# Perceiver block on one core: row loads issued ahead of the given chunks, statistics two tiles later, a third bank for the turned keys

## Time and profile before

| | us |
|---|---|
| median of 3 runs (lowest, highest) | 682.21 (680.39, 685.39) |
| the profiled execution | 680.11 |
| its span, first to last instruction | 678.4 |
| PE busy | 590.3 |
| DVE busy | 416.3 |
| ACT busy | 218.7 |
| POOL busy | 194.1 |
| granted TensorE clock, mean | 0.945 |

### The profile page before, as it was taken

The page is one execution under the profiler, slowest core; times in us unless marked ns, Lnnn a source line. Parts: engine busy times, 40 slices in busy tenths (PEclk is TensorE's granted clock), DMA queues, the critical chain, the costliest instruction groups (busy, mean ns, idle before and its releaser), DMA issues.

```text
span 678.4 us, 13117 instructions
## 1 busy us (share of the span) xinstructions
PE 590.3 (87%) x5217; PEld 365.4 (54%) x5217; DVE 416.3 (61%) x1026; ACT 218.7 (32%) x515; POOL 194.1 (29%) x259
## 2 busy tenths in 40 slices
PE   6999978979797978899687889999999999998778
PEld 5654444434343433444375576674958567584645
DVE  3967577867777685873658564563828264473732
ACT  0321231616252532233121243251516234151412
POOL 0423386775867576550000000101000010101010
PEclk9999969979897989799897799999999999999989
DMA  8960789593979776659606301203030301203000
GB/s 305 374 213 0 272 349 349 188 359 125 394 254 369 256 287 236 238 190 370 236 30 188 93 2 63 49 1 111 1 95 16 94 18 61 50 2 99 13 16 15
DMA packets 58972, 108.24 MB, mean 160 GB/s; under 512 B 19984, under 2 KB 22560, under 8 KB 56864
## 3 DMA queue, kind: packets, MB, share of 16 engines
q1 hardware_dynamic: 58912, 107.41, 45.4%
HBM read 96.91 MB, written 10.49 MB: 158 GB/s over the span
## 4 chain that ended last, share of the span: by engine, by line
PE 42%; issue 33%; DMA 8%; DVE 8%; POOL 3%; ACT 3%; SPq 1%; DVEq 0%; ACTq 0%; POOLq 0%
PE u_ps L878 8%; PE s_ps L852 7%; DMA area<-in_ctx_dram 7%; PE bank L943 3%; PE bank L817 3%; PE s_ps L725 2%; PE bank L1023 2%; PE max_ps L867 2%; PE s_ps L758 2%; DVE area L1396 1%; POOL area L491 1%; DMA area<-in_L_xattn_ln_b_dram 1%; DVE area L1117 1%; PE bank L1053 1%; PE max_ps L1023 1%
## 5 line engine op out<-in xcount | busy, mean ns | idle before, releaser
L1117 DVE BATCH_NORM_STATS2 area<-area 128x6 f32<-128x384 f32 (+1 forms) x208 | 104.2, 542 | 25.4 <-DMA area<-in_ctx_dram 25.4
L491 POOL TENSOR_SCALAR area<-area 128x384 f32<-128x384 f32 (+1 forms) x160 | 105.9, 673 | 10.3 <-POOL area L484 10.3
L878 PE MATMUL u_ps<-area,yT_all 128*64 128x384 f32 (+1 forms) x416 | 85.1, 539 | 0.7 <-ACT yT_all L609 0.7
L484 POOL TENSOR_TENSOR area<-area,minus_half 128x4 f32<-128x4 f32 (+1 forms) x56 | 56.2, 1003 | 99.9 <-DVE area L1126 99.9
L527 POOL TENSOR_TENSOR area<-area,minus_half 128x1 f32<-128x1 f32 x8 | 4.3, 539 | 240.0 <-DVE area L1390 240.0
L852 PE MATMUL s_ps<-area 128*64 128x512 f32 x288 | 69.9, 622 | 0.0
L999 PE MATMUL u_ps<-area 128*128 128x512 f16 x256 | 60.5, 386 | 0.0
L583 ACT COPY area<-bank 128x384 f32<-128x384 f32 (+1 forms) x80 | 32.1, 455 | 60.0 <-PE bank L817 60.0
L1412 DVE COPY area<-s_ps 128x512 f32<-128x512 f32 x8 | 5.5, 691 | 69.3 <-PE s_ps L1011 69.3
L878 PEld LDWEIGHTS u_ps<-area,yT_all 128*64 128x64 f32 (+1 forms) x416 | 27.5, 145 | 32.1 <-issue 30.4
L852 PEld LDWEIGHTS s_ps<-area 128*64 128x64 f32 x288 | 22.0, 148 | 41.5 <-issue 40.7
(11 more groups left out here) (181 smaller groups left out, 1021.2 us busy)
## 6 DMA issues: line engine op xcount, KB each, us to landing
area<-in_ctx_dram SPq DMA_DIRECT2D x96, 384.0 KB, 7.3
area<-in_ctx_turned_dram SPq DMA_DIRECT2D x32, 768.0 KB, 7.0
area<-in_L_ffn_W_turned_dram SPq DMA_DIRECT2D x16, 1024.0 KB, 8.7
skew<-area SPq DMA_DIRECT2D x8, 1024.0 KB, 4.3
area<-skew SPq DMA_DIRECT2D x16, 256.0 KB, 4.7
x_sb<-in_x_dram SPq DMA_DIRECT2D x8, 256.0 KB, 8.4
out_dram<-area SPq DMA_DIRECT2D x8, 256.0 KB, 2.0
area<-in_ctx_dram SPq DMA_DIRECT2D x16, 97.5 KB
```

The lines of the kernel that those rows point to most:

```text
L484: pool.tensor_tensor(rs[b][:, sl], ve[b][:, sl], minus_half[:, 0:n], ALU.pow).then_inc(s["rstd_ready"], 1)
L491: pool.tensor_scalar(raw[b][0:m, u, j, :], raw[b][0:m, u, j, :], negmu[b][0:m, i:i + 1], rs[b][0:m, i:i + 1], ALU.add, ALU.mult).then_inc( ...
L878: ins = pe.matmul(u_ps[u * L:(u + 1) * L, 0:DC], pT[0:m, j % NSLOT, u * L:(u + 1) * L], raw[b][0:m, u, j, :], start=(j == 0), stop=(j == N ...
L1117: dve.bn_stats(st[b][0:m, stat_at(u, j), :], raw[b][0:m, u, j, :]).then_inc(s["key_stats_done"], 1)
```

## The change

- SP issues the given chunk 2 of pair p - 1 not ahead of k = 0 of pair p, but behind its k = 1; the given chunk 1 of p goes behind k = 4 instead of k = 2. Of the last pair, chunk 2 is issued behind the loop.
- LEAD becomes 4 and STATS_AT [2, 2, 2, 2, 1, 2, 2]: step 0 does tiles 4 and 5, steps 1 to 3 the same tiles as before, step 4 tile 12 alone, step 5 tiles 0 and 1 of the next pair, step 6 tiles 2 and 3.
- The turned tiles rotate through three banks; the third is the bank of the factors. A turn waits for the copy three before it. A turn into the third bank also waits until the factors of the earlier pair (for tile 12: of this pair) are copied out, and the spreading of factors waits until the eight turns of chunk 0 are copied out.

```diff
-    LEAD = 6
+    LEAD = 4
-    STATS_AT = [0, 2, 2, 2, 2, 2, 3]
+    STATS_AT = [2, 2, 2, 2, 1, 2, 2]
...
-        tbank = [bank[0], bank[1]]
+        tbank = [bank[0], bank[1], s_ps[:, 1536:2048]]
...
-            load_given(1, 2)
             for p in range(2, NP):
                 for k in range(NL):
                     load_next(p, k)
-                    if k == 2:
+                    if k == 1:
+                        load_given(p - 1, 2)
+                    if k == 4:
                         load_given(p, 1)
                     if p in (4, 5) and k in (2, 5):
                         load_for_sum(2 * p - 4 + (k - 2) // 3)
-                load_given(p, 2)
+            load_given(NP - 1, 2)
...
-                             tbank[i % 2][:, 0:KC * P]...
+                             tbank[i % 3][:, 0:KC * P]...
...
-                    at_least(pe, s["turned_copied"], i - 1)
+                    at_least(pe, s["turned_copied"], i - 2)
+                    if i % 3 == 2:
+                        if p == 0:
+                            pe.wait_ge(s["cq_sums"], NT)
+                        at_least(pe, s["factors_copied"], len(GIVEN) * (p + (j == FT)))
...
                 pe.wait_ge(s["rstd_ready"], NB * p + 2 * ch + 2)
+                pe.wait_ge(s["turned_copied"], 2 * (len(TURNED) * p + len(TURNED) - 1))
                 at_least(pe, s["factors_copied"], i)
```

More of the change, by code:

```diff
@@ L583, in evacuate @@
                     act.copy(slot(j // CH)[:, u, :, (j % CH) * P:(j % CH) * P + m],
-                             tbank[i % 2][:, 0:KC * P].rearrange("p (c k) -> p c k", c=KC)[:, :, 0:m]).then_inc(s["turned_copied"], 1)
+                             tbank[i % 3][:, 0:KC * P].rearrange("p (c k) -> p c k", c=KC)[:, :, 0:m]).then_inc(s["turned_copied"], 1)
             def factors_out(p, ch):
@@ L814, in turn @@
                         pe.wait_ge(s["key_normed"], POOL_NORMS * p + 3 * g + 2 * (j % 2) + u + 1)
-                    at_least(pe, s["turned_copied"], i - 1)
+                    at_least(pe, s["turned_copied"], i - 2)
[3 more added lines that the diff above has]
+                        at_least(pe, s["factors_copied"], len(GIVEN) * (p + (j == FT)))
                     for c in range(KC):
-                        ins = pe.transpose(tbank[i % 2][:, c * P:c * P + m], raw[b][0:m, u, j, c * P:(c + 1) * P], ident_f[0:m, 0:m])
+                        ins = pe.transpose(tbank[i % 3][:, c * P:c * P + m], raw[b][0:m, u, j, c * P:(c + 1) * P], ident_f[0:m, 0:m])
                     ins.then_inc(s["key_turned"], 1)
```

## The result

| | before | after |
|---|---|---|
| median of the runs, us | 681.74 (680.39 to 685.39, 4 runs) | 652.62 (650.78 to 654.40, 4 runs) |
| profiled execution, us | 680.11 | 650.78 |
| its span, us | 678.4 | 649.1 |
| granted TensorE clock, mean | 0.945 | 0.966 |

The ratio of the times, after to before, is 0.9565, with a 95% interval of 0.9515 to 0.9615. A second timing of the same kernel gave 650.60 us and 0.9534 (0.9491 to 0.9577). The forecast was 650 and faster.

The account below looks back on a forecast made before the run. PE was taken as nearly the bound, with 6.4 us per pair lost preparing the next pair. Savings of 32.8 and 2.5 us less 4.2 gave 31.1, so 680.1 became 649.0 profiled, stated as 650 median; forecast 643 to 656, range 641 to 666.

Parts of the forecast that it names:

- What bounds the kernel: Pairs' loop: PE nearly the bound; preparing the next pair adds about 6.4 us per pair in waits and slow clock.
- The stall of 3.2 us: PE at L867: starts 3.2 us late because statistics waiting for rows precede chunk 1's maximum; moving them later removes it.
- DVE's step 0, no cost: DVE's step 0: an added 2.6 us statistics group costs nothing; context copy done at T + 7.5 instead of T + 7.2.
- The third bank, 0.3 us: PE's turned tiles: a third bank removes two 0.39 us waits per pair, counted as 0.3 us; bounds 0 to 0.8.
- The given chunk, 0.7 us in each of six stretches: PE before scoring chunk 2, stretches 1 to 6: new 0.7 us wait each, 4.2 in all; bounds 0 to 1.5.
- The sum: Whole run: 32.8 us from pairs 2 to 7, 2.5 from pair 1, less 4.2 for chunk waits: 31.1 us saved.
- The other signs: Trace after: L867 wait under 1 us, DVE's row wait below 8, stretches about 27.5, clock above 0.97, chunk wait near 4.
- (a): Rival, chance 0.16: DVE becomes the bound, its own norms held by POOL, 2.2 us per pair lost: 663 us.
- (b): Rival, chance 0.11: rows still late, k = 3 and given chunk slip 2 to 3 us per pair: 665 us.
- (c): Rival, chance 0.05: given chunk 2 lands so late that its wait exceeds the gain, slower: 689 us.
- (d): Rival, chance 0.05: nothing moves, chunk 1's maximum waits for the factors' copy instead: 678 us.
- (e): Rival, chance 0.05: better, no wait for the given chunk and pair 1 fully regained: 641.5 us.

Follow-up runs that it names:

- experiment 10: Changed kernel with STATS_AT = [2, 1, 3, 2, 1, 2, 2] and given chunk 2 issued behind k = 0: 644.51 us; the same with two banks: 647.69 us.
- the two experiments with one edit each: Kernel before with only the new LEAD and STATS_AT: 659.57 us; kernel before with only the new order of loads: 658.80 us.
- experiment 5: Changed kernel with the loads in their old order, keeping the later statistics and third bank: 669.02 us, ratio 0.9853.
- Experiment 7: Changed kernel with STATS_AT = [2, 1, 3, 2, 1, 2, 2], one tile instead of two ahead of step 1's context copy: 647.36 us, ratio 0.9523.
- experiment 8: Changed kernel with the given chunk 2 issued behind k = 0 instead of k = 1: 647.95 us, ratio 0.9535.
- experiment 6: Changed kernel with two banks for the turned keys instead of three: 652.44 us, ratio 0.9570.
- experiments 3: Kernel before with the third bank alone, and the waits that belong to it: 675.48 us, ratio 0.9920.
- experiment 9: Changed kernel with the given chunk 2 issued behind k = 2 instead of k = 1: 676.84 us, ratio 0.9911.

## Why the prediction was right

*What bounds the kernel.* Right. The time of a stretch without a next pair was the measure of what the others could reach, and experiment 10 reaches it within 0.3 us.

*The stall of 3.2 us.* Right, and the two experiments with one edit each show that either removes it. The prediction put it down to the statistics' place and counted nothing for the loads but their price. That was half of it: in experiment 5, with the old order, DVE waits 1.0 to 3.3 us for k = 3 in four of the stretches. The prediction had no term for this; of chunk 1's new place it said only "lands 10 us early".

*DVE's step 0, no cost.* The moment was right, the price wasn't, and this is where one of the prediction's own signs of being wrong came: DVE's context copy stands among what PE waits for, 8.6 us in seven. PE in stretches 3 and 4 of the kernel after:

```profile
149.12 0.80 PE L906 MATMUL max_ps<-ident_f,area 128*128 128x128 f32 x3 [1.17 <-DVE area L1258]
...
178.58 0.52 PE L906 MATMUL max_ps<-ident_f,area 128*128 128x128 f32 x3 [1.76 <-DVE area L1258]
```

Stretch 3 starts at 141.63, so the context is turned at T + 7.49, where T + 7.5 was forecast, and so it is in five of the stretches 2 to 7; stretch 4 starts at 170.55 and is late, at T + 8.03. Of that 0.5 us, 0.3 is a short DVE instruction (L1132) that takes 0.48 us instead of 0.17, until POOL's norms end. But a longer wait there isn't only its own time. After stretch 3's the clock is down, at 1.2 GHz:

```profile
150.00:151.00 1.00, 1.00 (x4) 0.39 (x6) 1.00 (x5) 1.00 (x2) 0.93 (x2) 0.50 0.25 55
```

That happened in stretches 3 and 5 (28.9 and 28.4 us, clock 0.94) and not in the others; in the second timing's profile it was stretches 3 and 4. The sum took the clock as 1.00 from stretch 2 on; this is the term that was too good, by about 3.2 us (PE busy 27.2 and 27.1 us in these two, 25.5 at the full clock). Experiment 7 takes 0.5 us off each of these waits, and the clock stays up in stretches 2 to 7, as it does in both kernels of experiment 10; in experiment 8, where the waits are as long as here, it falls in stretches 2 and 5. That supports the link. But experiment 8 and the three-bank kernel of experiment 10 have the clock at 0.88 in stretch 1, where no context is turned, so this wait is not all that a fall can come behind; and why waits of 1.2 us are followed by a fall in two stretches of six and not in the rest is not explained.

*The third bank, 0.3 us.* Right in stretch 7 (26.9 us without it in experiment 6, 26.6 with it), for the reason given: DVE's context copy caps it. The whole time can't show so small a term. Without the cap it is 0.7 (stretch 7 of experiments 3 and 10). "The new waits cost nothing" was wrong for pair 0, whose tile 12 comes right behind the spreading of chunk 2's factors, with no probabilities to turn and no tiles to weight in between:

```profile
84.36 0.37 PE L822 MATMUL s_ps<-ident_f,area 65*128 65x65 f32 x3 [0.78 <-ACT area L592]
```

*The given chunk, 0.7 us in each of six stretches.* Right in kind, 2.9 us instead of 4.2: three waits, of 0.62, 0.44 and 1.81 us, the last in stretch 4 with its weight pieces. The chain of waits shows that one: SP needs 0.8 us for k = 1, from 186.06, and 1.9 us (of which 1.37 for its first DMA) for the chunk, where it needed 0.93 in the case that the prediction reckoned from, and the chunk is in 10.5 us after k = 1 was issued, not 8.9.

```profile
186.90 1.37 SPq L367
...
188.32 8.21 DMA area<-in_ctx_turned_dram
```

*The sum.* Start of stretch 1: 0.8 us later than forecast by pair 0's wait, and 1.0 by the start of the run. Pair 1: 26.9 instead of 32.7, all 5.8 us regained where 2.5 were counted, less 0.7; 3.5 of the 5.8 are PE's busy time at a clock of 1.00 instead of 0.84. Stretches 2 to 7: 193.4 to 167.6, 25.8 us against the 29.3 forecast (32.8 less five chunk waits); the clock in stretches 3 and 5 is nearly all of the difference. Behind the loop 0.5 us more. Together 29.3 us against 31.1. That these lie so close is in part luck: pair 1 gave 4.0 us more than its terms, and everything else 5.8 us less. The last step of the prediction's sum is also off: 649.0 and the 2.1 us of the median over the profiled execution are 651.1, not 650; the medians measured are 652.62 and 650.60.

*The other signs.* PE's wait at L867 for ACT's copy of the probabilities is gone, DVE waits 0.6 us for rows, the clock of stretches 2 to 6 is 0.98 and the wait for the chunk 2.9 us, all as forecast; the stretches last 28.2 us where 27.5 was said.

*The rivals.* (a) came true in one place only, at the context copy. Busy DVE wasn't the bound: 24.6 us in a stretch of 28.2, and 24.6 in 26.5 in experiment 10. Nor were its own norms held up more often: in stretches 2 to 7 the 36 of the kernel before took 22.3 us, the longest 1.39, and after the change the 35 in the trace took 16.5 us, none above 0.48. POOL holds up another instruction instead, DVE's addition of eps to the variances (L1132): 40 took 7.1 us before and 15.0 after. (b) fell with the change's own load order; experiment 5 is (b) with the old one. (c) is experiment 9 in small: the chunk's wait of 3.4 us a stretch, where 5.9 was the point at which all would be lost, leaves 5 us of the gain. By the prediction's sum 15 should be left (35.3 less 20.2): its price of a wait left out the clock. (d) fell, since L867's wait went and the time with it. (e) had pair 1 right, fully regained; the chunk's wait was not nothing, and 641.5 was not reached even in experiment 10.

## What to carry to other kernels

Compare a stage with its last round, which prepares nothing: the difference is what preparation costs, and if the busy time of the engine that bounds both is alike, as PE's is here but for the clock, order alone may win it back. A wait for a load belongs behind the work that others wait for on the same engine; when it is moved, look at the next such piece (here the context copy) and at every load that now has less cover, not only at the first: a stall that goes away was cover for the loads behind it. In one queue each transfer's place is a price: 768 KB put ahead of the wanted chunk added 2.9 us of wait to each round, and moving the chunk one place forward cost nothing.

## What the runs showed that was not expected

DVE can be held by POOL for longer than one of POOL's instructions. In stretch 3 of the kernel after POOL runs two passes over `x_sb`, 2.51 us together, and DVE's addition of eps to 128 x 4 values, which takes 0.17 us elsewhere, takes 1.70 us until they end:

```profile
164.29 2.51 POOL L504 TENSOR_TENSOR x_sb<-x_sb,area 128x512 f32<-128x512 f32 x2
```

```profile
165.12 1.70 DVE L1132 TENSOR_SCALAR area<-area 128x4 f32<-128x4 f32 x1
```

DVE had the time to spare there; in stretch 4's step 1, told above, a shorter one of 0.3 us put off the context copy. The own norm of the earlier trace rows was the shorter case. The Trainium skill (SBUF — State Buffer, SBUF: two separate sides) says that the loser of the shared port pair blocks for the other's whole instruction; the trace agrees, and shows the block reaching past the end of one instruction of 1.25 us into the next.
